# GpSimd's residual DMAs issued behind VectorE's clamp, and a new order at the end of a wkv and binary-FFN kernel

## The chip, the cores and the metric

The kernel runs on one core of a Trainium2 chip. The metric is the device time of one execution in microseconds, the median of the runs shown. PE is TensorE, DVE is VectorE, ACT is ScalarE, POOL is GpSimd, SP is SyncE, which only issues DMAs. All arithmetic on data is in 32-bit floats except the operands of the large matmuls.

## The reference, cut to what matters

```python
x: (4, 1024, 1024); k = v = fside: (4, 1024, 1024)      # batch, time, channel
decay = exp(-exp(w)) * (0.5 + 0.5 * tf)                 # tf = sigmoid(sum(time_emb))
ek = exp(min(k, 30));  ekv = ek * v
nf, df = scan forward  (a = a * decay + ekv,  b = b * decay + ek)
nb, db = scan backward (the same)
euk = exp(min(u + k, 30))
num = nf + nb - ekv + euk * v
den = df + db - ek + euk
wkv = sigmoid(x) * num / max(den, 1e-8) * (0.8 + 0.2 * tf)
bw  = where(weight >= 0, 1, -1) * mean(|weight|, row)
out = x + wkv @ bw.T + bias
```

## The kernel before

**Tiles and steps.** One step n handles one tile of 128 channels by 1024 times; there are 4 batches of CT = 8 tiles, so N = 32 steps, n = 0 to 31. The rows of the profile repeat once per step, some 14.8 us apart. Batches 0 to 2 (24 tiles, 48 half tiles or units, `LAST = 24`) go through the output product inside the step loop, LAG = 9 steps behind; batch 3 is done in natural layout after the loop, in what is called the tail here.

**One step on each engine.** All names with n are semaphores that count finished operations.

- PE transposes k into PSUM `kT` (`k_turn`, 8 matmuls, it waits for VectorE's `own(n-1)`), x into `sT` (`s_turn`), and multiplies units of the product (`unit(u)`, 16 matmuls 128x512) and transposes them back (`turned(u)`, 4 matmuls into `yT`).
- VectorE, in this order: clamp(n) (L715, `pair` to `pair`, both in SBUF), val(n) (L721), own(n) (L722), two forward scans (L683), start values (L696), the backward scan of the numerator, yn(n) (L704), gate(n-1) (L740), the backward scan of the denominator, yd(n) (L704), den(n) (L745, `min(euk, .) + ek`, two inputs in SBUF). L721, L722 and L740 have one input in PSUM.
- ScalarE: ln and rec(n-1), the first guess of 1/den (L556, L558), hi and hib(n-2), the upper half of wkv as a 16-bit float and back (L565, L567), evacuations `evac(u)` (L535) and copies `y_copy(u)` (L544, into `o_nat`), two(n-1) (L591), the exponentials of step n+1 (L524, L525), and in even steps the sigmoids of two x tiles between two loads of activation tables (L607, L609).
- GpSimd: the DMA `ekv += own` of step n-1 (L322), chk(n-1) = euk * rec (L326), which waits for rec(n-1), inv(n-1) (L335), which waits for ScalarE's two(n-1), lo(n-2) (L301), and base(n-1) (L345, wkv times the numerator), which waits for gate(n-1). Clamp(n+1) waits for base(n-1) in turn.

**Residual DMAs.** `residuals(tiles)` (L314) issues on GpSimd, for every finished tile m, a DMA that adds x to `o_nat[m % 4]`. `summed(n)` says which tiles step n takes: none before step 11, one in steps 11 to 31, except steps 27 and 29, which take two (tiles 16 and 17, and 19 and 20), and tile 23 after the loop. Before, the first one stands between chk and inv, the second one behind lo and ahead of base; in steps 17 and 25 (`first`) the order is chk, lo, inv, residual, base. `biases(q)` (L307) issues the DMA that adds the bias to row block q of x, one in each of the steps 3 to 8, behind lo; its x block was loaded by SP (L242) one step earlier. SP stores a tile (L248) once its residual has landed.

**The order of ScalarE's product work** is set by two functions. `made(n)` is how many units PE has multiplied by step n, `cleared(n)` how many ScalarE has evacuated; `clear(lo, hi)` does evac(u) and y_copy(u-1) for each. Before, cleared(29) = 45, cleared(30) = 47, cleared(31) = 48, so evac(47) and y_copy(46) come in step 31, and y_copy(47) after the loop, ahead of `early_out(0)`.

**The tail.** The 16 half rows v of the last batch each need 8 tiles of 2 matmuls, 16 matmuls in all (`across(v, bank, tiles, ...)`). Tiles 0 to 4 are ready early, tile 5 once lo(29) is done, tile 6 with lo(30), tile 7 with `last_lo`. Before the wait on `last_lo` PE does what it can: v = 0 to 7 in the eight banks of PSUM, and v = 8 and 9 into bank 4 (`yT`), from which ScalarE copies them to SBUF (`early_out(0)` and `early_out(1)`, L572). After `last_lo` come the rest, v = 0 to 15 in order. ScalarE's `inverse(31)` (L556, L558) stands behind `early_out(0)`. VectorE ends chk, inv, gate, base and lo of tile 31 itself (L751 to L761), and then scales each half row (L772) and adds x and bias (L776); SP stores each full row block (L285).

Of the kernel before, what the change touches and what calls it, by code (L numbers as in the profile page):

```python
# [39 lines left out]
def bi_wkv_binary_ffn(nc, x, k, cond, w, u, weight, bias, out):  # L40
# [16 lines left out]
    def made(n):  # L57
        return 0 if n < LAG else LATE.get(n, 2 * LAST) if n > N - CT else 2 * (n - LAG + 1)

    def cleared(n):  # L60
        return 0 if n < LAG else made(n) - 1 if n < N - 1 else 2 * LAST

    copied = {u - 1: n for n in range(N) for u in range(cleared(n - 1), cleared(n))}
    copied[2 * LAST - 1] = N - 1
# [7 lines left out]
    with ExitStack() as ctx:  # L72
# [152 lines left out]
        @block.sync  # L225
        def _(sp):
            for p in range(NO):
                sp.sem_inc(o_out[p], 16)
            for i, a in enumerate((w, u, bias)):
                sp.dma_start(rows[i * CT:(i + 1) * CT, :], a.rearrange("(c p) -> c p", p=P)).then_inc(s_par, 16)  # L230
            sp.dma_start(cond4[:, :], cond).then_inc(s_cond, 16)
            sp.wait_ge(s_par, 48)
            sp.wait_ge(s_cond, 16)
            sp.dma_start(k_nat[1][:, :, :], tile_of(k, 1)).then_inc(k_in[1], 16)

            def load_x(n):

                sp.dma_start(x_nat[n % NX][:, :, :], tile_of(x, n)).then_inc(x_in[n % NX], 16)

            def load_tail(q):  # L240

                sp.dma_start(x_tail(q), natural(x, q)).then_inc(t_in[q], 16)  # L242

            def stores(n):
                for m in summed(n):

                    sp.wait_ge(res_in[m % NO], m // NO * 16 + 16)
                    sp.dma_start(tile_of(out_, m), o_nat[m % NO][:, :, :]).then_inc(o_out[m % NO], 16)  # L248

            load_x(0)  # L250
            load_x(1)

            def step(n, p, wt, nxt, nxt3, mid, low, out):
                if wt:

                    done(sp, "sgn", n - 2)
                    done(sp, "abs", n - 2)
                    sp.dma_start(w_nat[p][:, :], weight.rearrange("(o p) i -> o p i", p=P)[n])\
                      .then_inc(w_in[p], 16)
                if n == 0:  # L260
                    load_x(2)
                stores(n - 1)
                if nxt3:

                    done(sp, "kT", n + 1)
                    sp.dma_start(k_nat[1 - p][:, :, :], tile_of(k, n + 3)).then_inc(k_in[1 - p], 16)
                if mid and n + 2 < N:

                    done(sp, "sT", n - 1)
                    load_x(n + 2)  # L270
                if 2 <= n < TT:
                    load_tail(n - 2)
                if n >= N - 2:

                    done(sp, "kT", n)
                    load_tail(TT - N + n)

            out_ = out
            run(None, step)
            stores(N - 1)  # L280
            stores(N)
            for q in range(TT):

                done(sp, "res", 2 * q + 1)
                sp.dma_start(natural(out_, q), x_tail(q)).then_inc(s_tail, 16)  # L285
            for p in range(NO):
                sp.wait_ge(o_out[p], 16 * LAST // NO + 16)
            sp.wait_ge(s_tail, 16 * TT)

        @block.gpsimd  # L290
        def _(pool):
# [25 lines left out]
            def step(n, p, wt, nxt, nxt3, mid, low, out):  # L317
                W, R = wkv[1 - p][:, :], rec[1 - p][:, :]
                if mid:

                    done(pool, "yn", n - 1)
                    pool.dma_start(ekv[1 - p], own[1 - p][:, :], accum_op=ALU.add).then_inc(num_in[1 - p], 16)  # L322

                    done(pool, "rec", n - 1)
                    done(pool, "lo", n - 3)
                    pool.tensor_tensor(W, euk[1 - p][:, :], R, ALU.mult).then_inc(st["chk"], 1)  # L326
                first = n % CT == 1
                if low and first:
                    low_half(n - 2, p)
                if not first:  # L330
                    residuals(summed(n)[:1])
                if mid:

                    done(pool, "two", n - 1)
                    pool.tensor_tensor(W, W, R, ALU.mult).then_inc(st["inv"], 1)  # L335
                if low and not first:
                    low_half(n - 2, p)
                residuals(summed(n) if first else summed(n)[1:])
                if 3 <= n <= TT:
                    biases(n - 3)  # L340
                if mid:

                    done(pool, "gate", n - 1)
# [13 lines left out]
        def _(pe):  # L357
# [123 lines left out]
            done(pe, "own", N - 1)  # L481
            for v in (2, 3):
                across(v, bank[v], range(CT - 3), True, False)
            done(pe, "lo", N - 3)
            for v in range(4):
                across(v, bank[v], range(CT - 3, CT - 2), False, False)
            done(pe, "yc", 2 * LAST - 1)
            across(8, bank[4], range(CT - 2), True, True).then_inc(st["early"], 1)
            s_turn(N - 1)
            pe.wait_ge(st["early_sb"], 1)  # L490
            across(9, bank[4], range(CT - 2), True, True).then_inc(st["early"], 1)
# [9 lines left out]
            for v in range(2 * TT):  # L501
                if v >= 8:
                    done(pe, "res", v - 8)
                tiles = range(CT - 2, CT) if v < 6 or v in (8, 9) else range(CT - 1, CT) if v < 8 else range(CT)
                across(v, bank[v % 8], tiles, v >= 8, True).then_inc(st["nat"], 1)

        @block.scalar
        def _(act):
# [70 lines left out]
            def step(n, p, wt, nxt, nxt3, mid, low, out):  # L579
# [5 lines left out]
                    halves(n - 2, p)  # L585
                if out:
                    clear(cleared(n - 1), made(n - 1))
                if mid:

                    done(act, "chk", n - 1)  # L590
# [30 lines left out]

            run(None, step)

            y_copy(2 * LAST - 1)
            early_out(0)
            inverse(N - 1, 1)
            done(act, "base", N - 2)
# [174 lines left out]
```

## Time and profile before

| | before |
|---|---|
| median of 3 runs | 543.86 us (543.37 to 544.97) |
| the profiled execution | 544.33 us, span of its trace 542.6 us |
| VectorE busy | 504.8 us, 93% |
| ScalarE, GpSimd busy | 378.4 us, 362.3 us |
| PE busy | 363.8 us, granted clock 0.837 on the mean |
| DMA moved | 92.64 MB, 171 GB/s |

Busy time is the sum of the engine's instructions. The chain of the work that ended last (part 4 of the page) lies on VectorE for 59% of the span, and another 22% of it is "issue", time in which the engine that is followed waited for nothing that the profile shows; from 481 us on it lies on PE. An instruction that waits for a port inside its own execution shows that wait as a longer duration and not as idle time before it.

### The profile page before, as it was taken

To read this page: it belongs to the slowest core of one execution; us is meant where nothing else is said; L and a number is where in the kernel's file an instruction comes from. 1 tells how busy PE (TensorE), PEld (TensorE's weight loads), DVE (VectorE), ACT (ScalarE), POOL (GpSimd) and SP (SyncE) were. 2 spreads that over 40 slices of the span, in tenths; PEclk is the share of its full clock that TensorE was granted. 3 is DMA by queue.
4 is the path that set the end of the run, shared out by engine and by line. 5 is a ranking of instruction groups with operands and counts; after the bars stand their busy time and mean duration, and the time that the engine had idled before them with its cause. 6 is when DMAs were issued, how large, how long until landed. Compare 5 with 4: busy or idle time off the path is not lost.

```text
span 542.6 us, 5454 instructions
## 1 busy us (share of the span) xinstructions
PE 363.8 (67%) x1803; PEld 224.1 (41%) x1803; DVE 504.8 (93%) x385; ACT 378.4 (70%) x415; POOL 362.3 (67%) x194
## 2 busy tenths in 40 slices
PE   2233333322578786786786798778799888759996
PEld 1123333312335544444443454554455444524442
DVE  4999999999999999999999999999999999994593
ACT  2849688585859697796969696978889595953100
POOL 0157676667677877777877788877877879873200
PEclk9975655556698798798899878878899999779999
DMA  6745677777633798788899788888779998982942
GB/s 192 196 136 175 195 185 182 206 200 194 155 97 102 148 194 173 163 206 160 157 192 194 153 177 182 185 185 180 180 134 193 216 200 148 195 169 65 185 164 117
DMA packets 125778, 92.64 MB, mean 171 GB/s; under 512 B 2844, under 2 KB 117560, under 8 KB 125752
## 3 DMA queue, kind: packets, MB, share of 16 engines
q0 software_dynamic: 30720, 33.56, 39.2%
q1 hardware_dynamic: 92952, 57.70, 36.0%
q10 hardware_dynamic: 2080, 1.05, 0.7%
q8 instruction: 15, 0.25, 0.2%
q14 instruction: 11, 0.09, 0.1%
HBM read 58.74 MB, written 16.78 MB: 139 GB/s over the span
## 4 chain that ended last, share of the span: by engine, by line
DVE 59%; issue 22%; PE 11%; POOL 5%; DVEq 1%; ACT 1%; DMA 1%; SPq 0%; ACTq 0%
DVE pair L683 25%; DVE pair L704 9%; DVE wkv L740 7%; DVE own L722 6%; POOL wkv L345 5%; DVE pair L721 4%; DVE pair L715 4%; PE sT L420 3%; PE kT L420 3%; PE yT L420 2%; PE prod L420 1%; DVE euk L745 1%; PE cols L420 1%; DVE y_start L696 1%; DMA cond<-in_cond_dram 1%
## 5 line engine op out<-in xcount | busy, mean ns | idle before, releaser
L385 PE MATMUL prod<-acts,sgn 128*128 128x512 f16 x768 | 181.3, 390 | 4.3 <-ACT orow L618 4.0
L704 DVE TENSOR_TENSOR_SCAN pair<-cols,y_start,pair 128x1024 f32<-128x1024 f32 x64 | 150.1, 2346 | 1.1
L363 PE MATMUL kT<-ident,k_nat 128*128 128x128 f32 x256 | 52.1, 371 | 147.1 <-DVE own L722 147.1
L683 DVE TENSOR_TENSOR_SCAN pair<-cols,pair 128x1024 f32<-128x1024 f32 x64 | 142.8, 2272 | 0.0
L326 POOL TENSOR_TENSOR wkv<-euk,rec 128x1024 f32<-128x1024 f32 x31 | 73.1, 2357 | 84.0 <-ACT rec L558 84.0
L385 PEld LDWEIGHTS prod<-acts,sgn 128*128 128x128 f16 (+1 forms) x768 | 77.4, 101 | 90.2 <-issue 9.6
L363 PEld LDWEIGHTS kT<-ident,k_nat 128*128 128x128 f32 x256 | 42.1, 192 | 158.5 <-issue 157.9
L556 ACT ACTIVATE rec<-euk,lnb 128x1024 f32<-128x1024 f32 x32 | 36.8, 1150 | 84.9 <-DVE euk L745 84.8
L335 POOL TENSOR_TENSOR wkv<-wkv,rec 128x1024 f32<-128x1024 f32 x31 | 72.9, 2350 | 18.1 <-ACT wkv L591 18.1
L345 POOL TENSOR_TENSOR wkv<-wkv,pair 128x1024 f32<-128x1024 f32 x31 | 74.1, 2392 | 11.5 <-DVE wkv L740 10.1
L301 POOL TENSOR_TENSOR acts<-wkv,rec 128x1024 f16<-128x1024 f32 x31 | 73.2, 2363 | 9.5 <-ACT rec L567 9.5
L363 PE MATMUL sT<-ident,x_nat 128*128 128x128 f32 x256 | 51.6, 370 | 0.0
L363 PEld LDWEIGHTS sT<-ident,x_nat 128*128 128x128 f32 x256 | 46.2, 199 | 0.4
L745 DVE SCALAR_TENSOR_TENSOR euk<-euk,pair 128x1024 f32<-128x1024 f32 x32 | 43.5, 1360 | 1.1
L363 PE MATMUL yT<-ident,y_fm 128*128 128x128 f32 x192 | 34.0, 307 | 12.3 <-ACT o_nat L544 11.6
L322 POOL DMA_DIRECT2D pair<-own x31 | 29.1, 939 | 19.2 <-DVE pair L704 19.2
L535 ACT ACTIVATE y_fm<-prod,bcol,oscale 128x512 f32<-128x512 f32 x48 | 37.2, 776 | 6.5 <-issue 5.6
L721 DVE TENSOR_TENSOR pair<-pair,kT 128x1024 f32<-128x1024 f32 x32 | 39.0, 1220 | 1.1 <-ACT euk L525 0.3
L591 ACT ACTIVATE wkv<-wkv,two 128x1024 f32<-128x1024 f32 x31 | 35.8, 1155 | 6.0 <-POOL wkv L326 6.0
L722 DVE SCALAR_TENSOR_TENSOR own<-euk,kT 128x1024 f32<-128x1024 f32 x32 | 38.8, 1213 | 0.0
L314 POOL DMA_DIRECT2D o_nat<-in_x_dram x24 | 38.0, 1582 | 0.0
L740 DVE SCALAR_TENSOR_TENSOR wkv<-wkv,sT 128x1024 f32<-128x1024 f32 x31 | 37.0, 1195 | 0.0
(88 smaller groups left out, 502.2 us busy)
## 6 DMA issues: line engine op xcount, KB each, us to landing
x_nat<-in_x_dram SPq DMA_DIRECT2D x32, 512.0 KB, 6.9
pair<-own POOLq DMA_DIRECT2D x32, 512.0 KB, 4.7
k_nat<-in_fside_BxSxS_dram SPq DMA_DIRECT2D x30, 512.0 KB, 3.5
o_nat<-in_x_dram POOLq DMA_DIRECT2D x24, 512.0 KB, 9.1
out_dram<-o_nat SPq DMA_DIRECT2D x24, 512.0 KB, 5.0
y_fm<-in_L_ffn_weight_dram SPq DMA_DIRECT2D x8, 512.0 KB, 5.7
x_end<-in_x_dram SPq DMA_DIRECT2D x6, 512.0 KB, 5.1
x_end<-in_L_ffn_bias_dram POOLq DMA_DIRECT2D x6, 512.0 KB, 6.0
```

What stands on the lines that cost most here:

```text
L301: pool.tensor_tensor(acts[:, 1, n % (2 * CT), :], wkv[p][:, :], rec[p][:, :], ALU.subtract)\
L326: pool.tensor_tensor(W, euk[1 - p][:, :], R, ALU.mult).then_inc(st["chk"], 1)
L335: pool.tensor_tensor(W, W, R, ALU.mult).then_inc(st["inv"], 1)
L345: pool.tensor_tensor(W, W, ekv[1 - p], ALU.mult).then_inc(st["base"], 1)
L363: ins = pe.transpose(dst(q), what(q), one)
L385: ins = pe.matmul(prod[:, h, :], view[:, c, m % CT * P:m % CT * P + P], acts[:, part, m // CT % 2 * CT + c, h * H:(h + 1) * H], start=(par ...
L420: ins = pe.matmul(dst, acts[:, part, LAST // CT % 2 * CT + c, v // 2 * P:(v // 2 + 1) * P], view[:, c, v % 2 * H:(v % 2 + 1) * H], start=( ...
L683: dve.tensor_tensor_scan(buf, d, buf, 0.0, ALU.mult, ALU.add).then_inc(st["F" + kind], 1)
L704: dve.tensor_tensor_scan(buf[:, ::-1], d, buf[:, ::-1], y_start[:, i:i + 1], ALU.mult, ALU.add)\
L721: dve.tensor_tensor(V, E, kT[:, :], ALU.mult).then_inc(st["val"], 1)
L722: dve.scalar_tensor_tensor(own[p][:, :], U, E30, kT[:, :], ALU.min, ALU.mult)\
L740: dve.scalar_tensor_tensor(W, W, HI_SCALE * LO_GAIN / DEN_MIN, sT[:, :], ALU.min, ALU.mult)\
```

## The change

Four things are changed.

1. On GpSimd the first residual DMA of a step now stands right behind the `ekv += own` DMA, with a new wait for clamp(n) ahead of it. The second one (steps 27 and 29), and no other, stands between chk and inv. The bias DMAs of steps 3 to 8 move from behind lo to the same early place, without a wait for the clamp.
2. `cleared(30)` becomes 48: evac(47) and y_copy(46) move to the end of ScalarE's step 30, and y_copy(47) moves into step 31, ahead of two(30).
3. On PE, half row 8 is begun as soon as y_copy(47) is done, with tiles 0 to 4 alone (10 matmuls in place of 12), ahead of the wait for lo(29); its tile 5 is done in the end, where v = 8 now has tiles 5 to 7.
4. The store of the last row block is issued as two halves of 512 columns, the first after half row 14, the second after half row 15.

```diff
     def cleared(n):
-        return 0 if n < LAG else made(n) - 1 if n < N - 1 else 2 * LAST
+        return 0 if n < LAG else made(n) - 1 if n < N - 2 else 2 * LAST
...
-            for q in range(TT):
+            for q in range(TT - 1):
                 done(sp, "res", 2 * q + 1)
                 sp.dma_start(natural(out_, q), x_tail(q)).then_inc(s_tail, 16)
+            for h in range(NH):
+                done(sp, "res", 2 * TT - 2 + h)
+                sp.dma_start(natural(out_, TT - 1)[:, h * H:(h + 1) * H], x_tail(TT - 1)[:, h * H:(h + 1) * H])\
+                  .then_inc(s_tail, 16)
...
                     pool.dma_start(ekv[1 - p], own[1 - p][:, :], accum_op=ALU.add).then_inc(num_in[1 - p], 16)
+                if summed(n):
+                    done(pool, "clamp", n)
+                    residuals(summed(n)[:1])
+                if 3 <= n <= TT:
+                    biases(n - 3)
+                if mid:
                     done(pool, "rec", n - 1)
...
-                if not first:
-                    residuals(summed(n)[:1])
+                residuals(summed(n)[1:])
                 if mid:
                     done(pool, "two", n - 1)
                     pool.tensor_tensor(W, W, R, ALU.mult).then_inc(st["inv"], 1)
                 if low and not first:
                     low_half(n - 2, p)
-                residuals(summed(n) if first else summed(n)[1:])
-                if 3 <= n <= TT:
-                    biases(n - 3)
...
+            done(pe, "yc", 2 * LAST - 1)
+            across(8, bank[4], range(CT - 3), True, True).then_inc(st["early"], 1)
             done(pe, "lo", N - 3)
             for v in range(4):
                 across(v, bank[v], range(CT - 3, CT - 2), False, False)
-            done(pe, "yc", 2 * LAST - 1)
-            across(8, bank[4], range(CT - 2), True, True).then_inc(st["early"], 1)
...
-                tiles = range(CT - 2, CT) if v < 6 or v in (8, 9) else range(CT - 1, CT) if v < 8 else range(CT)
+                tiles = range({6: CT - 1, 7: CT - 1, 8: CT - 3}.get(v, CT - 2) if v < 10 else 0, CT)
...
                     clear(cleared(n - 1), made(n - 1))
+                if n == N - 1:
+                    y_copy(2 * LAST - 1)
                 if mid:
...
             run(None, step)
-            y_copy(2 * LAST - 1)
             early_out(0)
```

GpSimd in step 27, which takes two residual DMAs, from one `ekv += own` DMA (`pair<-own`) to the next. `o_nat<-in_x_dram` is a residual, the four others are chk, inv, lo and base in this order. Before:

```order
L322 DMA pair<-own 128x1024
L326 TENSOR_TENSOR wkv<-euk,rec 128x1024
L314 DMA o_nat<-in_x_dram 128x8x128
L335 TENSOR_TENSOR wkv<-wkv,rec 128x1024
L301 TENSOR_TENSOR acts<-wkv,rec 128x1024
L314 DMA o_nat<-in_x_dram 128x8x128
L345 TENSOR_TENSOR wkv<-wkv,pair 128x1024
L322 DMA pair<-own 128x1024
```

and after:

```order
L327 DMA pair<-own 128x1024
L319 DMA o_nat<-in_x_dram 128x8x128
L338 TENSOR_TENSOR wkv<-euk,rec 128x1024
L319 DMA o_nat<-in_x_dram 128x8x128
L346 TENSOR_TENSOR wkv<-wkv,rec 128x1024
L306 TENSOR_TENSOR acts<-wkv,rec 128x1024
L353 TENSOR_TENSOR wkv<-wkv,pair 128x1024
L327 DMA pair<-own 128x1024
```

Both residuals have moved one place up: the first now runs ahead of chk, the second ahead of inv, and nothing stands between lo and base.

ScalarE from the second table load of step 30 to the first part of `inverse(31)`, with evac (`y_fm<-prod`), y_copy (`o_nat<-yT`), two (`wkv<-wkv,two`) and early_out (`y_fm<-yT`). Before:

```order
L609 ACT_TABLE_LOAD
L556 ACTIVATE rec<-euk,lnb 128x1024
L558 ACTIVATE rec<-rec 128x1024
L565 ACTIVATE acts<-wkv 128x1024
L567 ACTIVATE rec<-acts 128x1024
L535 ACTIVATE y_fm<-prod,bcol,oscale 128x512
L544 COPY o_nat<-yT 128x512
L591 ACTIVATE wkv<-wkv,two 128x1024
L544 COPY o_nat<-yT 128x512
L572 COPY y_fm<-yT 128x512
L556 ACTIVATE rec<-euk,lnb 128x1024
```

and after:

```order
L619 ACT_TABLE_LOAD
L543 ACTIVATE y_fm<-prod,bcol,oscale 128x512
L552 COPY o_nat<-yT 128x512
L564 ACTIVATE rec<-euk,lnb 128x1024
L566 ACTIVATE rec<-rec 128x1024
L573 ACTIVATE acts<-wkv 128x1024
L575 ACTIVATE rec<-acts 128x1024
L552 COPY o_nat<-yT 128x512
L601 ACTIVATE wkv<-wkv,two 128x1024
L580 COPY y_fm<-yT 128x512
L564 ACTIVATE rec<-euk,lnb 128x1024
```

The last evacuation and the copy of unit 46 have moved ahead of the first guess of tile 30, and the copy of unit 47 ahead of two.

PE from the transpose of x tile 30 (`sT<-ident,x_nat`) to the long product of v = 6 and 7 (`sT<-sgn,acts`, 28 matmuls). Before:

```order
L363 MATMUL sT<-ident,x_nat 128x128 x8
L363 MATMUL yT<-ident,y_fm 128x128 x4
L420 MATMUL prod<-sgn,acts 128x512 x10
L420 MATMUL kT<-sgn,acts 128x512 x20
L420 MATMUL prod<-sgn,acts 128x512 x4
L420 MATMUL kT<-sgn,acts 128x512 x4
L420 MATMUL yT<-sgn,acts 128x512 x12
L363 MATMUL sT<-ident,x_nat 128x128 x8
L420 MATMUL yT<-sgn,acts 128x512 x12
L420 MATMUL cols<-sgn,acts 128x512 x12
L420 MATMUL yT<-sgn,acts 128x512 x12
L420 MATMUL sT<-sgn,acts 128x512 x28
```

and after:

```order
L371 MATMUL sT<-ident,x_nat 128x128 x8
L371 MATMUL yT<-ident,y_fm 128x128 x4
L428 MATMUL prod<-sgn,acts 128x512 x10
L428 MATMUL kT<-sgn,acts 128x512 x20
L428 MATMUL yT<-sgn,acts 128x512 x10
L428 MATMUL prod<-sgn,acts 128x512 x4
L428 MATMUL kT<-sgn,acts 128x512 x4
L371 MATMUL sT<-ident,x_nat 128x128 x8
L428 MATMUL yT<-sgn,acts 128x512 x12
L428 MATMUL cols<-sgn,acts 128x512 x12
L428 MATMUL yT<-sgn,acts 128x512 x12
L428 MATMUL sT<-sgn,acts 128x512 x28
```

Half row 8 (the first `yT<-sgn,acts`) has moved ahead of the 8 matmuls that wait for lo(29), and is two matmuls shorter.

## Rows read from the trace of the kernel before

**Rows 1.** The page, part 1: busy time, share of the span, instructions.

```profile
PE 363.8 (67%) x1803; PEld 224.1 (41%) x1803; DVE 504.8 (93%) x385; ACT 378.4 (70%) x415; POOL 362.3 (67%) x194
```

**Rows 2.** The instructions of L745, den: duration in ns min/median/max.

```profile
L745 DVE SCALAR_TENSOR_TENSOR euk<-euk,pair x32: 1224/1226/3369, 22.9 to 489.3; 128x1024 f32<-128x1024 f32 x32
```

**Rows 3.** Timeline (start us, us, instruction, idle before), steps 27 and 29.

```profile
417.95 1.59 POOL L314 DMA_DIRECT2D o_nat<-in_x_dram  x1
...
419.87 2.35 POOL L335 TENSOR_TENSOR wkv<-wkv,rec 128x1024 f32<-128x1024 f32 x1 [0.33 <-ACT wkv L591]
...
422.19 2.36 POOL L301 TENSOR_TENSOR acts<-wkv,rec 128x1024 f16<-128x1024 f32 x1
...
424.50 1.54 POOL L314 DMA_DIRECT2D o_nat<-in_x_dram  x1
425.47 2.96 POOL L345 TENSOR_TENSOR wkv<-wkv,pair 128x1024 f32<-128x1024 f32 x1
426.15 3.37 DVE L745 SCALAR_TENSOR_TENSOR euk<-euk,pair 128x1024 f32<-128x1024 f32 x1
...
457.72 3.35 DVE L745 SCALAR_TENSOR_TENSOR euk<-euk,pair 128x1024 f32<-128x1024 f32 x1
```

**Rows 4.** Timeline, step 26, one residual.

```profile
396.73 1.23 DVE L745 SCALAR_TENSOR_TENSOR euk<-euk,pair 128x1024 f32<-128x1024 f32 x1
397.89 0.74 DVE L715 TENSOR_SCALAR pair<-pair,scl 128x1024 f32<-128x1024 f32 x1
...
400.33 2.36 POOL L326 TENSOR_TENSOR wkv<-euk,rec 128x1024 f32<-128x1024 f32 x1 [2.60 <-ACT rec L558]
...
403.31 1.16 ACT L591 ACTIVATE wkv<-wkv,two 128x1024 f32<-128x1024 f32 x1
...
409.23 2.36 POOL L345 TENSOR_TENSOR wkv<-wkv,pair 128x1024 f32<-128x1024 f32 x1
...
411.45 1.23 DVE L745 SCALAR_TENSOR_TENSOR euk<-euk,pair 128x1024 f32<-128x1024 f32 x1
```

**Rows 5.** Timeline, end of step 3 and start of step 4, weights still being read.

```profile
65.15 0.87 POOL L307 DMA_DIRECT2D x_end<-in_L_ffn_bias_dram  x1
65.16 1.20 DVE L740 SCALAR_TENSOR_TENSOR wkv<-wkv,sT 128x1024 f32<-128x1024 f32 x1
...
68.64 1.23 DVE L745 SCALAR_TENSOR_TENSOR euk<-euk,pair 128x1024 f32<-128x1024 f32 x1
68.73 0.86 POOL L322 DMA_DIRECT2D pair<-own  x1
69.79 0.75 DVE L715 TENSOR_SCALAR pair<-pair,scl 128x1024 f32<-128x1024 f32 x1
```

**Rows 6.** Timeline from step 31 to the first half row of the tail.

```profile
475.82 1.15 ACT L556 ACTIVATE rec<-euk,lnb 128x1024 f32<-128x1024 f32 x1 [0.57 <-DVE euk L745]
...
481.38 1.08 PE L363 MATMUL yT<-ident,y_fm 128*128 128x128 f32 x4 [5.70 <-ACT o_nat L544]
...
489.27 1.23 DVE L745 SCALAR_TENSOR_TENSOR euk<-euk,pair 128x1024 f32<-128x1024 f32 x1
...
494.88 0.59 ACT L572 COPY y_fm<-yT 128x512 f32<-128x512 f32 x1 [11.79 <-PE yT L420]
...
497.63 1.23 DVE L751 SCALAR_TENSOR_TENSOR wkv<-euk,rec 128x1024 f32<-128x1024 f32 x1 [7.13 <-ACT rec L558]
...
499.54 0.57 ACT L572 COPY y_fm<-yT 128x512 f32<-128x512 f32 x1
...
500.73 2.75 PE L420 MATMUL yT<-sgn,acts 128*128 128x512 f16 x12
...
505.63 1.22 DVE L761 TENSOR_TENSOR acts<-wkv,rec 128x1024 f16<-128x1024 f32 x1 [2.21 <-ACT rec L567]
```

**Rows 7.** Busy time by stretch: start:end, length, PE, PEld, DVE, ACT, POOL, clock, DMA, GB/s.

```profile
515.57:538.10 22.53, 22.45 (x105) 9.99 (x102) 16.32 (x26) 0.00 (x0) 0.00 (x0) 1.00 0.36 145
538.10:542.60 4.50, 0.00 (x0) 0.00 (x0) 1.35 (x2) 0.00 (x0) 0.00 (x0) 0.73 0.29 117
```

More of the change, by code:

```diff
@@ L281, in _ @@
             stores(N)
-            for q in range(TT):
+            for q in range(TT - 1):
                 done(sp, "res", 2 * q + 1)
                 sp.dma_start(natural(out_, q), x_tail(q)).then_inc(s_tail, 16)
+            for h in range(NH):
+                done(sp, "res", 2 * TT - 2 + h)
+                sp.dma_start(natural(out_, TT - 1)[:, h * H:(h + 1) * H], x_tail(TT - 1)[:, h * H:(h + 1) * H])\
+                  .then_inc(s_tail, 16)
             for p in range(NO):
                 sp.wait_ge(o_out[p], 16 * LAST // NO + 16)
-            sp.wait_ge(s_tail, 16 * TT)
+            sp.wait_ge(s_tail, 16 * TT + 16)
         @block.gpsimd
```

## The prediction

> **What bounds the kernel now.** I read the busy table first: VectorE is busy 93% of the span, ScalarE, GpSimd and PE about 70% [rows 1]. So inside the steps a gain must come out of VectorE's own instructions or their waits. The instructions by line then show one oddity: den (L745) takes 1.226 us at the median of 32 and 3.369 at most [rows 2]. The timeline has just two such, 3.37 us at 426.15 and 3.35 us at 457.72 [rows 3]; they are the ends of steps 27 and 29, the two with two residual DMAs. There base (L345) ends at 425.47 + 2.96 = 428.43, and den at 429.52, 1.09 us later. In step 26 base ends at 411.59 (409.23 + 2.36) [rows 4]; 1.09 us on is 412.68, just when den ends there undisturbed (411.45 + 1.23). So den, two inputs in SBUF, doesn't read while GpSimd's base reads, and pays for a late base one for one; in all other steps base ends just in time.
>
> In the end VectorE waits: 7.13 us before its chk of tile 31 [rows 6]. That hangs on ScalarE, which sat 11.79 us before `early_out(0)`, from 483.1 to 494.88, for PE, though den(31) had ended at 489.27 + 1.23 = 490.50 and `inverse(31)` stood behind that copy [rows 6]. PE was late as it had idled 5.70 us before turning unit 47 at 481.38, for y_copy(46) [rows 6]. From there PE works on to 538.1: it is 22.45 of 22.53 us busy in the last long stretch, at full granted clock [rows 7]. That stretch is v = 8 to 15 by the program, 4 + 4 + 6 x 16 = 104 matmuls, so 0.2166 us each.
>
> **Part 1, second residual.** In steps 27 and 29 it leaves the place between lo and base. Lo ends at 422.19 + 2.36 = 424.55, so base runs to 426.91 and den, 1.09 later, ends at 428.00 in place of 429.52: 1.52 us. It isn't the whole 2.14, since GpSimd is some 0.6 us late there anyway. Step 29 gives as much. The residual now stands where the first one stood: it ran from 417.95 to 419.54 there, under the wait for two(n-1) that let inv start at 419.87 [rows 3], so it costs nothing. **-3.04 us.** Bounds: 2.4 if base starts 0.3 later each time, 4.3 if den is never disturbed.
>
> **Part 1, first residual** (21 steps, 11 to 31). It leaves a place where inv waits for ScalarE in any case (0.33 us after it [rows 3]): no gain. In its new place, behind the clamp, it starts about 0.08 us after 398.63 (397.89 + 0.74) and needs 1.59, to 400.30; chk started at 400.33 after 2.60 us of waiting [rows 3, 4]. It just fits. Should it be late, chk ends at 402.69 and ScalarE comes to two at 403.31 [rows 4], so 0.6 us more is free. The copies it needs lie in the step before. Queued behind the new wait is chk alone. It now runs beside val and own, which have one input in PSUM like gate (L740), and a DMA issue of GpSimd ran beside gate with 1.20 and 0.87 us for the two [rows 5]. **0 us**, bounds -0.2 and +2 (0.1 in 21 steps).
>
> **Part 1, bias DMAs** (steps 3 to 8). Issued right behind L322 they would run from about 69.6 to 70.5 beside the clamp, at 69.79 to 70.54, while chk comes some 3.6 us after den's start, as at 400.33 after 396.73, so at 72.2 [rows 4, 5]. GpSimd has room for a delay up to 1.7 us. Whether VectorE's clamp is held up no row shows: no DMA issue of GpSimd overlaps a clamp in this trace. The nearest row is L322 at 68.73 beside den at 68.64, with 0.86 and 1.23 us, neither longer than alone [rows 2, 5]. I take **0 us** by that row; the other end is 70.46 less the clamp's real start at 69.87, 0.59 us each, 3.5 us for six.
>
> The Trainium skill speaks against this half: its page "SBUF — State Buffer", section "Who interferes with whom", says that a `tensor_scalar` in a 2-port mode takes the pair of ports shared with GpSimd, that descriptor writing needs them, and that issue order decides who blocks. The clamp is a `tensor_scalar` of 0.75 us, where the same 1024 elements cost den 1.23, so it may well be in such a mode; den has two inputs, for which the page names only GpSimd's reads. By it den beside L322 proves nothing for the clamp, and the sum would be 3.5 us worse; no run here shows it yet.
>
> **Part 2, the end.** ScalarE was free at 475.25 (0.57 us before 475.82 [rows 6]). Evac(47) and y_copy(46) take 1.15 us with their overlap, so ln(30) starts at 476.40, 0.58 late. In step 31 only y_copy(47) stands between hib and two(30) instead of those two, so two(30) keeps its time within 0.1 us, and the rest of step 31 too. PE can turn unit 47 at about 476.55, 4.83 earlier. Its work then, at 0.2166 us per matmul: v = 1 to 479.2, v = 2, 3 to 483.5, the 10 matmuls of v = 8 to 485.7. So `early_out(0)` is over at 486.3, before den(31) ends at 490.50, and ln(31) starts at 490.54 in place of 495.36: all of VectorE's and ScalarE's chain moves 4.82 earlier (chk from 497.63 to 492.8).
>
> PE meanwhile waits for lo(29) at 487.05 (lo ends as base starts, 2.22 before den, by 409.23 and 411.45 [rows 4]), and does its 8 matmuls, x tile 31, v = 9 and v = 5 until 494.9. Then it waits for `early_out(1)`, which was at 499.54 and comes at 494.72 to 495.29. So the 12 matmuls at 500.73 [rows 6] start at 495.4: 5.33 earlier. Nothing behind is later than that: `last_lo`, 506.85 before (505.63 + 1.22), comes at 502.03, while v = 6, 7 keep PE until 504.0. The tail is PE's as before, plus 2 matmuls of v = 8: 0.43 us. **-5.33 + 0.43 = -4.90 us.** If PE runs at half clock for the first ten matmuls, its waits swallow nearly all of it: -4.8. VectorE waited several times in the last rows and stays hidden.
>
> **Part 4, last store.** The DMAs moved for 0.29 of 4.50 us after PE's end [rows 7], 1.3 us for 512 KB; half remains, as the first half goes out 3.4 us earlier. **-0.65 us**, bounds 0 and -1.3.
>
> **Sum.** -3.04 + 0 + 0 - 4.90 - 0.65 = -8.6 us. The profiled execution was 544.33, so 535.7; it stood 0.47 above the median of 543.86, so **535.3**.
>
> **Rivals.**
>
> - *Clamp held up by the bias DMA.* Six times 0.59 = 3.5 us, all on VectorE: 538.8. For it: 0.75 us for the clamp against 1.23 for den shows that the two read differently, so den beside L322 says little. Against it: that pair is still the nearest row, and GpSimd could as well be the one that waits, for free. 20%. The Trainium skill's rule above points the same way, with the order of issue, GpSimd first, as its reason.
> - *The end stays PE's.* If PE doesn't get ahead at 481, because y_copy(46) or own(31) come later than I think, part 2 gives 0 and costs the two matmuls: 535.3 + 4.9 + 0.43 = 540.6. Against it: own(31) ends near 478.9 (den(30) near 475.8, then clamp, val and own, 0.74 + 2 x 1.2, the latter like gate), and ScalarE's free moment is in the rows. 7%.
> - *Slower: GpSimd becomes the bound through the residual's new place.* If descriptor writing beside val and own took twice as long, 3.18 us, chk would come 3.18 - 1.59 - 0.03 = 1.56 late, two 0.96 after its 0.6 of slack, and base is just in time, so den pays 0.96 in each of 21 steps: 20 us, 555.5. It ends slower than 543.9 from a duration of about 2.65 us on, since 8.6 / 21 = 0.41 a step. For it: lo, base and den follow without slack, as steps 27 and 29 show. Against it: gate beside L307. 7%.
> - *It doesn't do what it says:* den at 426 is long for another reason than base, and PE hides the rest: within 0.3%, 3%.
>
> **How the numbers follow.** The forecast gets 63%, with a range of its own of 533.8 to 536.8 (den never disturbed -1.2 and the store's bound; +0.6 and +0.65 the other way, and 0.1 in some steps). The range for 8 in 10 adds the held clamp: 533.8 to 539.2; outside it lie the tail that stays, the slower case and the one without effect, 17%. What a measurement of this kernel can tell from no change is about 0.3%, 1.6 us. Faster: 63 + 20 + 7 = 90%; same: 3%; slower: 7%.
>
> **What the profile after would show.** Den at steps 27 and 29: about 1.8 us each, not 3.4 (1.23 would mean that I have base too late). In steps 3 to 8 clamps of 0.75 as before; clamps of 1.3 would be the first rival. GpSimd's idle time before chk falls from 2.6 to nearly 0 without a later chk. PE turns unit 47 some 4.8 us before the place that it had relative to den(31), no more wait of ScalarE ahead of ln(31), and the first half row of the tail about 5.3 earlier relative to den(31). The stretch after PE's end falls from 4.5 to 3.9 us. I would be wrong if GpSimd's chk were late in most steps, or if the clamps grew.

## The result and the profile after

The changed kernel takes 535.14 us on the median of 4 runs (534.97 to 535.84), the kernel before 543.92 (543.37 to 544.97): a ratio of 0.9839, 95% interval 0.9821 to 0.9856, or 8.8 us less. The profiled execution took 535.84 us, the longest of the four; its span is 534.0 us against 542.6.

Line numbers have moved: on GpSimd chk is now L338, inv L346, lo L306, base L353, the residual L319 and the bias L312, on VectorE the clamp is L724 and den L754, on ScalarE early_out is L580, and `across` on PE is L428.

The four answers below are den's, the clamp's and the bias DMA's instructions, with their duration in ns (min/median/max), and the sign instruction's. The sign instruction turns a tile of the weights into signs; one stands right behind the clamp in each of the steps 0 to 7. They answer to [rows 2] and [rows 5].

```profile
L754 DVE SCALAR_TENSOR_TENSOR euk<-euk,pair x32: 1224/1225/1778, 22.9 to 486.2; 128x1024 f32<-128x1024 f32 x32
L724 DVE TENSOR_SCALAR pair<-pair,scl x32: 740/744/753, 9.8 to 472.7; 128x1024 f32<-128x1024 f32 x32
L312 POOL DMA_DIRECT2D x_end<-in_L_ffn_bias_dram x6: 1359/1359/1362, 54.0 to 130.6; - x6
L698 DVE TENSOR_SCALAR o_nat<-y_fm x8: 665/722/725, 17.5 to 116.5; 128x1024 f16<-128x1024 f32 x8
```

The timeline of GpSimd and VectorE through steps 26 and 27 (start us, us, instruction, idle before) answers to [rows 3, 4]:

```profile
399.06 1.57 POOL L319 DMA_DIRECT2D o_nat<-in_x_dram  x1 [1.21 <-DVE pair L724]
400.45 2.57 POOL L338 TENSOR_TENSOR wkv<-euk,rec 128x1024 f32<-128x1024 f32 x1
404.68 2.36 POOL L346 TENSOR_TENSOR wkv<-wkv,rec 128x1024 f32<-128x1024 f32 x1 [1.65 <-ACT wkv L601]
...
418.08 1.55 POOL L319 DMA_DIRECT2D o_nat<-in_x_dram  x1
420.00 2.35 POOL L346 TENSOR_TENSOR wkv<-wkv,rec 128x1024 f32<-128x1024 f32 x1 [0.37 <-ACT wkv L601]
422.31 2.36 POOL L306 TENSOR_TENSOR acts<-wkv,rec 128x1024 f16<-128x1024 f32 x1
424.64 2.34 POOL L353 TENSOR_TENSOR wkv<-wkv,pair 128x1024 f32<-128x1024 f32 x1
```

```profile
396.87 1.23 DVE L754 SCALAR_TENSOR_TENSOR euk<-euk,pair 128x1024 f32<-128x1024 f32 x1
...
426.29 1.77 DVE L754 SCALAR_TENSOR_TENSOR euk<-euk,pair 128x1024 f32<-128x1024 f32 x1
```

Base follows lo at once in step 27 and den is 1.60 us shorter than its 3.37. The residual in its early place ends at 400.63. Chk's row begins at 400.45, inside that of the residual, and is 0.21 us longer than the 2.36 of [rows 4], so chk ends 6.15 us after den's start where it had ended after 5.96. These 0.19 us vanish before inv, which waits 1.65 us for two.

The end, on ScalarE, PE and VectorE, answers to [rows 6]:

```profile
473.37 1.16 ACT L564 ACTIVATE rec<-euk,lnb 128x1024 f32<-128x1024 f32 x1
...
473.62 0.63 PE L371 MATMUL yT<-ident,y_fm 128*128 128x128 f32 x4 [0.99 <-ACT o_nat L552]
...
480.57 2.32 PE L428 MATMUL yT<-sgn,acts 128*128 128x512 f16 x10
...
482.93 0.58 ACT L580 COPY y_fm<-yT 128x512 f32<-128x512 f32 x1 [3.68 <-PE yT L428]
...
492.30 2.76 PE L428 MATMUL yT<-sgn,acts 128*128 128x512 f16 x12 [0.31 <-ACT y_fm L580]
494.90 6.21 PE L428 MATMUL sT<-sgn,acts 128*128 128x512 f16 x28
500.94 1.89 PE L428 MATMUL prod<-sgn,acts 128*128 128x512 f16 x8
```

```profile
486.24 1.22 DVE L754 SCALAR_TENSOR_TENSOR euk<-euk,pair 128x1024 f32<-128x1024 f32 x1
489.77 1.22 DVE L760 SCALAR_TENSOR_TENSOR wkv<-euk,rec 128x1024 f32<-128x1024 f32 x1 [2.30 <-ACT rec L566]
...
502.00 0.70 DVE L781 TENSOR_TENSOR prod<-prod,orow 128x512 f32<-128x512 f32 x1 [3.01 <-PE prod L428]
...
530.06 0.70 DVE L781 TENSOR_TENSOR sT<-sT,orow 128x512 f32<-128x512 f32 x1 [1.96 <-PE sT L428]
530.79 0.69 DVE L785 TENSOR_TENSOR k_nat<-sT,k_nat 128x512 f32<-128x512 f32 x1
```

PE idles 0.99 us before unit 47 where it had idled 5.70, the first early_out is over before den(31) begins, and VectorE waits 2.30 us before chk, the time that ScalarE's ln and rec of tile 31 take, where it had waited 7.13. The end of the trace comes 2.52 us after VectorE's last instruction (531.48 to 534.0), against 3.12 before. The rows of the kernel before that mark the start of the tail on PE and VectorE's last half row are these:

```profile
509.37 1.89 PE L420 MATMUL prod<-sgn,acts 128*128 128x512 f16 x8
...
538.06 0.70 DVE L772 TENSOR_TENSOR sT<-sT,orow 128x512 f32<-128x512 f32 x1 [1.96 <-PE sT L420]
```

### The profile page after: what moved, and what is told of

The parts are those of the page before. It is cut to its first block, busy times and chain, and to the rows that moved or that the text cites. A ratio compares the mean times of both kernels' runs of the same rounds, so it can differ in the third digit from the quotient of the medians.

```text
span 534.0 us, 5476 instructions
## 1 busy us (share of the span) xinstructions
PE 361.6 (68%) x1803; PEld 222.9 (42%) x1803; DVE 501.8 (94%) x385; ACT 378.5 (71%) x415; POOL 365.0 (68%) x194
## 4 chain that ended last, share of the span: by engine, by line
DVE 61%; issue 23%; PE 8%; POOL 5%; DVEq 1%; ACT 1%; DMA 1%; SPq 0%; ACTq 0%
DVE pair L692 26%; DVE pair L713 10%; DVE wkv L749 7%; DVE own L731 7%; POOL wkv L353 5%; DVE pair L730 5%; DVE pair L724 4%; PE sT L428 3%; PE kT L428 2%; PE yT L428 1%; DVE y_start L705 1%; DVE euk L754 1%; PE cols L428 1%; PE prod L428 1%; DMA cond<-in_cond_dram 1%
## 5 line engine op out<-in xcount | busy, mean ns | idle before, releaser
L346 POOL TENSOR_TENSOR wkv<-wkv,rec 128x1024 f32<-128x1024 f32 x31 | 73.6, 2374 | 39.2 <-ACT wkv L601 39.2
L338 POOL TENSOR_TENSOR wkv<-euk,rec 128x1024 f32<-128x1024 f32 x31 | 78.2, 2524 | 23.0 <-ACT rec L566 23.0
L353 POOL TENSOR_TENSOR wkv<-wkv,pair 128x1024 f32<-128x1024 f32 x31 | 72.9, 2353 | 19.0 <-DVE wkv L749 17.5
L306 POOL TENSOR_TENSOR acts<-wkv,rec 128x1024 f16<-128x1024 f32 x31 | 74.0, 2388 | 4.6 <-ACT rec L575 4.6
L319 POOL DMA_DIRECT2D o_nat<-in_x_dram x24 | 37.8, 1576 | 26.7 <-DVE pair L724 26.7
L754 DVE SCALAR_TENSOR_TENSOR euk<-euk,pair 128x1024 f32<-128x1024 f32 x32 | 40.3, 1260 | 1.1
L327 POOL DMA_DIRECT2D pair<-own x31 | 27.6, 891 | 19.2 <-DVE pair L713 19.2
```

The costliest lines, as they stand in the source:

```text
L306: pool.tensor_tensor(acts[:, 1, n % (2 * CT), :], wkv[p][:, :], rec[p][:, :], ALU.subtract)\
L353: pool.tensor_tensor(W, W, ekv[1 - p], ALU.mult).then_inc(st["base"], 1)
L754: dve.scalar_tensor_tensor(U, U, E30, E, ALU.min, ALU.add).then_inc(st["den"], 1)
```

## The experiments

Each ratio compares a run with the kernel before on the same chip, whose median was 543.92 to 544.86 us. Where a time is set beside the changed kernel's 535.14 us, the two were not measured together, and a difference under 1 us tells nothing, since the medians of the kernel before differ by as much.

### One part at a time

`p1_res_alone` is the kernel before with GpSimd's moves alone. 

> The kernel before with the moves of the residual and bias DMAs on GpSimd alone. Theory: den of steps 27 and 29 falls from 3.37 and 3.35 to 1.77 us, all other dens stay at 1.23, and the bias DMAs cost about 0.14 us together, so the time falls by 3.0 us, to 540.9 with before at 543.9, and VectorE still waits 7.1 us before its chk of tile 31. Rival: the moves do more than that by shorter landings (6.2 us in place of 9.1 in the changed kernel), which would show as a fall of over 4 us; or the steps' gain is given back at the end, under 2 us.

Measured: 540.83 us against 544.15, ratio 0.9929 (0.9905 to 0.9953), 3.3 us less. So the shorter landings, which came here too (6.4 us for the residuals), bring nothing of their own that shows. Two details missed: in the profiled execution (542.51 us, the longest of four) den took 2.17 us in step 27 and 1.77 in step 29, and VectorE's wait before chk of tile 31 was 7.77 us and not 7.1. The 2.17 comes from chk, which begins 4.80 us after den(26) where the changed kernel has 4.18, as it waits for rec; why ScalarE is later there is open.

`p2_end_alone` has ScalarE's and PE's orders alone:

```diff
-        return 0 if n < LAG else made(n) - 1 if n < N - 1 else 2 * LAST
+        return 0 if n < LAG else made(n) - 1 if n < N - 2 else 2 * LAST
...
+                if n == N - 1:
+                    y_copy(2 * LAST - 1)
...
-            y_copy(2 * LAST - 1)
             early_out(0)
...
+            done(pe, "yc", 2 * LAST - 1)
+            across(8, bank[4], range(CT - 3), True, True).then_inc(st["early"], 1)
             done(pe, "lo", N - 3)
...
-            done(pe, "yc", 2 * LAST - 1)
-            across(8, bank[4], range(CT - 2), True, True).then_inc(st["early"], 1)
...
-                tiles = range(CT - 2, CT) if v < 6 or v in (8, 9) else range(CT - 1, CT) if v < 8 else range(CT)
+                tiles = range({6: CT - 1, 7: CT - 1, 8: CT - 3}.get(v, CT - 2) if v < 10 else 0, CT)
```

> The kernel before with ScalarE's and PE's new order at the end alone (parts 2 and 3), the store whole. Theory: -4.9 us, to 539.0: ln(31) starts right behind den(31), VectorE's wait before chk of tile 31 falls from 7.1 to 2.3 us, the 12 matmuls ahead of the 28 start 5.3 us earlier, and the tail is 0.43 us longer by two matmuls. Den of steps 27 and 29 stays at 3.4. Rival: with the dens still long the ScalarE order gives another amount, as steps 27 and 29 are the ones that set GpSimd's and ScalarE's distance there: under 4 us.

Measured: 539.28 us, ratio 0.9899 (0.9874 to 0.9924), 4.9 us less; the wait before chk is 2.31 us, den still takes 3.37 at most. The two add up to 8.2 of 8.8 us, each with some 1.3 us of uncertainty. The store was not run alone, but the traces show it: from VectorE's last instruction to the end it is 3.09 to 3.16 us in the six with the whole store (the kernel before, p1 to p4, q3), and 2.48 to 2.56 in the seven with the two halves.

`p3_act_alone` is the first three pieces of that diff (ScalarE's order), `p4_pe_alone` the last three (PE's).

> The kernel before with ScalarE's new order alone, PE in its old order. Theory, from the changed kernel's rates: PE turns unit 47 some 4.8 us earlier but waits for lo(29) before v = 8, which then ends near den(31) + 0.9 us, so ln(31) starts some 1.5 us after den(31) ends, and all behind it too. The tail starts about 2.1 us later than with both and is 0.43 us shorter: -3.2 us, to 540.7. Rival: ScalarE's order is the whole of it, and PE's order gives nothing: -4.9.

> The kernel before with PE's new order alone, ScalarE in its old one. Theory: PE still turns unit 47 at 481.4 and works without a gap from there to 538, so that moving two matmuls behind and one group ahead changes nothing at the end: within 0.4 us of before, though ln(31) starts about 2.1 us earlier and VectorE's wait before chk falls from 7.1 to 5.0 us. Rival: VectorE's chain sets the end, and the time falls by about 2 us with it.

Measured: p3 542.54 us on the median of 10 runs (540.76 to 544.13), ratio 0.9961 (0.9947 to 0.9976), 1.6 us less and not 3.2. p4 544.07 us, ratio 0.9993 (0.9980 to 1.0006): nothing, as expected, though VectorE's wait before chk fell from 7.1 to 5.6 us there (5.0 expected), and its wait for the first half row rose from 3.58 to 5.29. So the end hung on PE and not on VectorE's chain. The shares aren't additive: 1.6 and 0 apart, 4.9 together. PE's timeline in p3's profiled execution, at 544.13 us the longest of its ten, shows one reason:

```profile
479.31 4.48 PE L420 MATMUL kT<-sgn,acts 128*128 128x512 f16 x20
...
487.39 1.89 PE L420 MATMUL prod<-sgn,acts 128*128 128x512 f16 x4 [3.60 <-POOL acts L301]
...
489.07 1.91 PE L420 MATMUL kT<-sgn,acts 128*128 128x512 f16 x4
...
490.78 3.78 PE L420 MATMUL yT<-sgn,acts 128*128 128x512 f16 x12
```

and the stretches of p3 (start:end, length, PE, PEld, DVE, ACT, POOL, granted clock, DMA, GB/s), the wait and what follows it:

```profile
483.70:487.30 3.60, 0.09 (x1) 0.00 (x0) 3.60 (x3) 0.00 (x0) 3.60 (x3) 0.82 1.12 142
487.30:490.70 3.40, 3.31 (x8) 1.20 (x9) 3.37 (x2) 0.00 (x0) 3.20 (x3) 0.50 0.54 154
490.70:494.30 3.60, 3.60 (x13) 1.47 (x12) 0.02 (x1) 0.00 (x0) 0.00 (x0) 0.70 0.77 146
```

Left without work for 3.60 us, PE comes back at a granted clock of 0.50, the lower of its two levels (1.2 GHz): the two groups of 4 matmuls take 1.9 us each where the changed kernel's take 1.0, and the 12 take 3.78 for 2.75. That is 2.8 us on the engine that sets the end. With both orders the ten matmuls of v = 8 fill most of that wait, and the clock stays at 1.00:

```profile
473.60:482.90 9.30, 9.26 (x44) 4.29 (x44) 9.16 (x7) 5.58 (x6) 7.51 (x4) 1.00 0.73 113
482.90:484.05 1.15, 0.01 (x1) 0.02 (x2) 1.15 (x2) 0.58 (x1) 1.11 (x2) 1.00 0.96 290
484.05:491.90 7.85, 7.85 (x40) 3.94 (x40) 5.48 (x4) 4.34 (x5) 3.22 (x3) 1.00 0.39 77
```

The runs of p3 lie 3.4 us apart, the fastest (540.76) just where my theory had it and the median 1.8 us above. That the clock doesn't fall, or falls for a shorter time, in some of them would fit, but one trace can't show it.

### Why den was long

`q3_den_psum`, on the kernel before, takes den's second SBUF input away in steps 27 and 29:

```diff
-                dve.scalar_tensor_tensor(U, U, E30, E, ALU.min, ALU.add).then_inc(st["den"], 1)
+                if isinstance(n, int) and n in (27, 29):
+                    done(dve, "expU", n + 1)
+                    dve.scalar_tensor_tensor(U, U, E30, kT[:, :], ALU.min, ALU.max).then_inc(st["den"], 1)
+                else:
+                    dve.scalar_tensor_tensor(U, U, E30, E, ALU.min, ALU.add).then_inc(st["den"], 1)
```

> The kernel before, with den of steps 27 and 29 taking its second input from kT in PSUM in place of ek in SBUF (max in place of the sum, so the denominators of these two tiles are other numbers), behind ScalarE's exponentials. Theory: den is long because its second SBUF input waits for base on GpSimd, so it falls to 1.23 us in both steps. The clamp behind it waits for base by a semaphore, so only part of the 2.1 us is won: clamp starts near base's end + 0.1, about 0.9 us earlier, 1.8 us in all, 542.1. Rival: den waits for something else that is late then (DMA issue, a queue), and stays at 3.4 us with the time of before.

```profile
425.42 2.97 POOL L345 TENSOR_TENSOR wkv<-wkv,pair 128x1024 f32<-128x1024 f32 x1
426.10 1.22 DVE L747 SCALAR_TENSOR_TENSOR euk<-euk,kT 128x1024 f32<-128x1024 f32 x1
...
428.50 0.75 DVE L715 TENSOR_SCALAR pair<-pair,scl 128x1024 f32<-128x1024 f32 x1 [1.17 <-POOL wkv L345]
```

Base is as late as before, yet den takes 1.22 us beside it: it was the second SBUF input that waited for GpSimd's instruction. The clamp then shows the same lateness openly, as 1.17 us of waiting. The time is 541.43 us against 544.13, ratio 0.9952 (0.9936 to 0.9969): 2.7 us and not 1.8. The two traces show where the rest is. Step 27 gives 0.95 us (clamp at 428.50 for 429.45), but step 29 gives 1.50: chk begins 3.59 us after den(28) there and not 4.18, so base ends 1.68 us after den's start in place of 2.27. And PE's ten matmuls after unit 47 took 3.45 us, where the profiled execution of the kernel before has 3.94 and that of p1 4.47. In all three PE had idled 5.1 to 6.3 us before, and over the first 4.6 to 4.7 us of this work the granted clock was 0.65, 0.55 and 0.50. So up to 1 us comes and goes there from run to run.

`q2_res_before_base` puts all residual DMAs where the second one had been, on the changed kernel:

```diff
-                if summed(n):
-                    done(pool, "clamp", n)
-                    residuals(summed(n)[:1])
...
-                residuals(summed(n)[1:])
...
                 if low and not first:
                     low_half(n - 2, p)
+                residuals(summed(n))
```

> The changed kernel with all residual DMAs between lo and base, where the second one of steps 27 and 29 stood before; the bias DMAs as in the changed kernel. Theory: base comes some 1.5 us late in each of the 21 steps and den is held as long, 2.6 to 3.4 us in place of 1.23, for some 30 us more, near 565. Rival: den was long in steps 27 and 29 for a reason of those steps (three units of the product in the step before, DMA traffic) and stays at 1.23 in the steps with one residual; then the time is within 5 us of 535.

Measured in a single run: 565.25 us, 30 more than the changed kernel.

```profile
L750 DVE SCALAR_TENSOR_TENSOR euk<-euk,pair x32: 1224/2646/4355, 22.7 to 514.7; 128x1024 f32<-128x1024 f32 x32
```

Half of all dens are now longer than 2.6 us, and each of the long ones that I compared ends 1.09 or 1.10 us after its base (base to 401.01, den to 402.10). Only in steps 17 and 25, where the order differs and base waits for gate in any case, is den 1.23 us. So den pays for a late base in any step, and steps 27 and 29 aren't special.

### What the wait for the clamp is for

`q1_no_clamp_wait` is the changed kernel without the line `done(pool, "clamp", n)`.

> The changed kernel without GpSimd's wait for the clamp: the first residual DMA follows the ekv DMA at once and so is issued beside the clamp. Theory: as the bias DMAs beside the clamp showed in the changed kernel (1.36 us for 0.87, clamp 0.75 as ever), VectorE isn't held and GpSimd is, by some 0.5 to 0.7 us; the residual then ends no later than it does behind the wait, chk is on time, and the time is that of the changed kernel within 0.5 us, 535.1. Rival A: the longer residual DMA holds the clamp, 0.4 us or more in 21 steps, over 8 us slower. Rival B: it is held far longer than the clamp lasts, chk comes late by more than 0.6 us, and den pays.

Measured: 546.41 us against 544.13, ratio 1.0042 (1.0025 to 1.0059), and 11.3 us slower than the changed kernel. My theory fell. The clamp's instructions, and one of them with the residual beside it:

```profile
L723 DVE TENSOR_SCALAR pair<-pair,scl x32: 744/1317/1340, 9.7 to 483.1; 128x1024 f32<-128x1024 f32 x32
```

```profile
421.43 2.18 POOL L319 DMA_DIRECT2D o_nat<-in_x_dram  x1
...
421.89 1.32 DVE L723 TENSOR_SCALAR pair<-pair,scl 128x1024 f32<-128x1024 f32 x1
```

Clamp 1.32 in place of 0.745 us: 0.57 in each of 21 steps is 12.0 us. Against that, no den is longer than 1.24 us here, which gives 1.1 back; den(31) begins 11.0 us later than in the changed kernel. Chk isn't late; it still waits 0.7 us for rec. So rival A holds. But the bias DMAs are issued in just that way beside the clamp and leave it at 0.75 us; between them and the residuals the pieces differ, 4 KB against 512 B. `q5_rows` is the kernel of q1 and changes only these:

```diff
-                    pool.dma_start(o_nat[m % NO][:, :, :], tile_of(x, m), accum_op=ALU.add)\
+                    pool.dma_start(o_nat[m % NO][:, :, :].rearrange("p q f -> p (q f)"),
+                                   x[m // CT, (m % CT) * P:(m % CT + 1) * P, :], accum_op=ALU.add)\
```

> As q1_no_clamp_wait (no wait for the clamp), but the residual DMA adds a block of 128 whole rows of x, 4 KB in a piece for each partition, in place of the 128x8x128 tile in pieces of 512 B: the same bytes, an eighth of the pieces, so a wrong residual in batches 0 to 2. Theory, formed on the run without the wait (clamp 1.32 us in place of 0.75 beside a residual issue of 2.18, but 0.75 beside a bias issue of 1.36): what holds the clamp is the writing of many pieces; with the bias DMA's number of them the issue takes 1.4 us, the clamp 0.75, and the time is near 535. Rival: it is the place in the step, or the batches' other work, and the clamp stays at 1.3 us, near 546.

Measured: 536.13 us, ratio 0.9851 (0.9811 to 0.9891).

```profile
398.13 1.34 POOL L319 DMA_DIRECT2D o_nat<-in_x_dram  x1
...
398.61 0.74 DVE L724 TENSOR_SCALAR pair<-pair,scl 128x1024 f32<-128x1024 f32 x1
```

The same bytes at the same place in 4 KB pieces: the clamp is 0.74 us and the 10 us are gone. So what holds VectorE goes with the pieces. In the changed kernel, where the small pieces are issued behind the clamp, val and own beside them keep their 1.22 and 1.21 us, so it matters that the issue meets the clamp. Whether the number of descriptors that GpSimd writes does it, their size or the first transfers, no run separates.

How long GpSimd is held is less than the durations say, since the row of an issue right behind another issue begins before that one ends. In q5's tail, with no clamp near, it begins 0.29 us early and shows 1.18 us:

```profile
495.05 0.88 POOL L319 DMA_DIRECT2D o_nat<-in_x_dram  x1
495.64 1.18 POOL L312 DMA_DIRECT2D k_nat<-in_L_ffn_bias_dram  x1
```

Counted from the end of the issue before, a bias DMA takes 0.89 us there and 1.08 beside the clamp (54.29 to 55.37 in the changed kernel), and q1's residual takes 1.89 (421.72 to 423.61) where one behind the clamp takes 1.57. GpSimd loses 0.2 and 0.3 us, VectorE nothing and 0.57.

The Trainium skill, page "SBUF — State Buffer", section "Who interferes with whom", says that the first of the two to start gets the shared ports for its whole instruction and the other blocks fully. Of den against base that holds here in each trace. Of the clamp against the residual DMA it holds in part: both grow, the DMA by 0.3 us and the clamp from 0.745 to 1.32, and the clamp ends at 423.21, before the DMA does, so neither was blocked for the whole of the other. The bias DMA begins before the clamp (54.29 and 54.50) and doesn't block it at all.

`q4_bias_old` is the changed kernel with the bias DMAs back behind lo.

> The changed kernel with the bias DMAs of steps 3 to 8 back behind lo. Theory: the bias DMAs take 0.87 us again, the sign instruction behind the clamp 0.69 in place of 0.72, and VectorE reaches step 26 some 0.14 us earlier; nothing that the time can show. Rival: the 0.14 us stays, as it has another cause.

Measured in one run: 535.61 us. The bias DMAs take 0.866 us, the sign instruction 0.685 where it had 0.722, and den of step 25 begins at 396.65 and not at 396.87. Of these 0.22 us, 0.12 stand there before the first bias DMA counts (den of step 2 at 53.23 and 53.35). The bias DMAs' place costs the changed kernel 0.10 to 0.14 us, and in each of the five steps with signs behind the clamp the sign instruction is 0.037 us longer. The rival falls.

### A faster version

`r1_two_first` is the changed kernel with ScalarE's two ahead of the first evacuation in steps 27 and 29:

```diff
-                if out:
+                if out and n not in (27, 29):
                     clear(cleared(n - 1), made(n - 1))
...
+                if out and n in (27, 29):
+                    clear(cleared(n - 1), made(n - 1))
                 if nxt:
                     exps(n + 1, 1 - p)
```

> The changed kernel with one more move on ScalarE: in steps 27 and 29 the first evac and y_copy come behind two. Theory: what is left of den there (1.77 and 1.78 us) is ScalarE's lateness after the three units of the step before; two now comes when chk ends, inv follows the second residual's end 0.35 us earlier than before, and den falls to about 1.4 us each: 0.7 us less in all, 534.4. Rival: evac's delay hits PE and comes back; no gain or a loss.

`r2_all` adds the bias DMAs' old place and a fuller PE at the end:

```diff
             across(8, bank[4], range(CT - 3), True, True).then_inc(st["early"], 1)
+            pe.wait_ge(st["early_sb"], 1)
+            across(9, bank[4], range(CT - 3), True, False)
             done(pe, "lo", N - 3)
+            across(9, bank[4], range(CT - 3, CT - 2), False, True).then_inc(st["early"], 1)
...
-            pe.wait_ge(st["early_sb"], 1)
-            across(9, bank[4], range(CT - 2), True, True).then_inc(st["early"], 1)
...
+            for v in (6, 7):
+                across(v, bank[v], range(CT - 2), True, False)
             done(pe, "lo", N - 2)
             for v in (6, 7):
-                across(v, bank[v], range(CT - 1), True, False)
+                across(v, bank[v], range(CT - 2, CT - 1), False, False)
...
             early_out(0)
+            early_out(1)
             inverse(N - 1, 1)
```

> As r1_two_first, with the bias DMAs back behind lo and PE's waits at the end filled: half row 9 begins with tiles 0 to 4 right behind early_out(0), its tile 5 comes with lo(29), early_out(1) comes ahead of inverse(31), and v = 6 and 7 take tiles 0 to 5 before they wait for lo(30). Theory: PE's waits of 1.1 us (lo(29)) and 0.3 us (early_out(1)) shrink to 0.5 in all, the tail starts 0.9 us earlier relative to den(31); with 0.7 and 0.14 from the steps 1.8 us in all, 533.3. Rival: VectorE's chain to last_lo takes over as the bound, or PE's clock falls; gain under 1 us.

Measured: r1 534.28 us, ratio 0.9813 (0.9797 to 0.9829), r2 533.13 us, ratio 0.9792 (0.9776 to 0.9808), against 544.86 for before. R1's interval overlaps the changed kernel's 0.9821 to 0.9856, so its gain isn't shown; in its profiled execution den of step 27 even took 2.17 us and that of step 29 1.44. As in p1, chk was late for rec in step 27, 5.01 us after den(26). R2 lies clear of it, by 2.0 us by the medians and 0.5% by the ratios. Its dens take 1.44 and 1.43 us as expected, and at the end:

```profile
485.29 1.23 DVE L759 SCALAR_TENSOR_TENSOR euk<-euk,pair 128x1024 f32<-128x1024 f32 x1
...
500.10 0.70 DVE L786 TENSOR_TENSOR prod<-prod,orow 128x512 f32<-128x512 f32 x1 [2.06 <-PE prod L428]
```

From den(31)'s end to the first half row it is 13.58 us, where the changed kernel has 14.54 (487.46 to 502.00): 0.96, for an expected 0.9.

## Why the prediction was right

The forecast was 535.3 us and the measured median 535.14. Its terms, each as the two profiled executions show it (that of the kernel before at 544.33 us, that of the changed one at 535.84):

| term | forecast | measured |
|---|---|---|
| den of steps 27 and 29 | -3.04 | 3.37 + 3.35 to 1.77 + 1.78: -3.17 |
| first residual's new place | 0 | 0 (inv 7.81 us after den, 7.83 before) |
| bias DMAs | 0 | den(25) at 396.87 for 396.73: +0.14 |
| end of den(31) to the start of the tail on PE | -5.33 | 18.87 to 13.48: -5.39 |
| two more matmuls: start of the tail on PE to VectorE's last L772 (now L781) | +0.43 | 28.69 to 29.12: +0.43 |
| last store: VectorE's end to the end | -0.65 | 3.12 to 2.52: -0.60 |
| sum | -8.6 | -8.6 (span 542.6 to 534.0) |

That the medians agree to 0.2 us is luck in part. The rows of den and of the bias DMAs miss by -0.13 and +0.14 and cancel; den of step 27 took 2.17 us in p1 and r1 against 1.77, and PE's ten matmuls after unit 47 took 3.45 to 4.47 us in kernels with ScalarE's old order, so either row could have come out 0.4 or 0.5 us off. One sum of the prediction is wrong without effect: 535.3 - 1.2 - 0.65 is 533.4 and not 533.8, the lower end of its range.

**Second residual.** That den pays one for one for a late base was read from two instructions; q3 (den without its second SBUF input: 1.22 us beside the same base) and q2 (30 us for residuals in that place in all steps) show it as the cause. That 0.6 us would stay was right (0.54 did). The prediction put it down to GpSimd, which is late in these steps anyway; what makes it late is ScalarE, whose rec lets chk begin 4.2 us after den's start in place of 3.6, and r2, with two in an earlier place, takes 0.34 of each den away.

**First residual.** It fitted, with 0.2 us less room than I had, out of the 0.6: the residual starts 0.30 us behind the clamp's end (399.06) and not 0.08. The slower rival, its issue stretched beside val and own, didn't come: it takes 1.57 us there. I hadn't seen what the wait for the clamp is worth: without it the move costs 11.3 us more and the kernel would have been slower than before (q1). My row for a DMA issue beside den, and later the bias DMAs beside the clamp, spoke for few large pieces alone.

**Bias DMAs.** The rival had six clamps held for 0.59 us each. The clamps stayed at 0.745 us and the issue's row grew to 1.36, of which 0.2 us is delay; 0.14 us came in the steps with sign instructions, which I had left out. The residual DMA shows that the rival was no idle one: 1024 pieces hold a clamp for 0.57 us. That this is near the rival's 0.59 is a coincidence, for that was the overlap with an issue of 0.87 us.

**The end.** The gain was PE's, as the prediction had it, with VectorE's chain moved 4.83 us for 4.82 (its wait from 7.13 to 2.30). P3 and p4 show that neither order does it alone. The prediction's remark that a half clock at the start would be swallowed didn't get its test, for the clock stayed at 1.00 in the changed kernel. In p3 it fell later, after the wait for lo(29), with no wait behind it, and cost 2.8 us.

## What to carry to other kernels

A VectorE instruction with two SBUF inputs beside GpSimd's elementwise work hides its wait in its own duration, so compare its longest with its median; a DMA issue of GpSimd is paid there by pushing the next elementwise instruction into it. Issue scattered DMAs from GpSimd outside an instruction like the clamp here (one input, both sides in SBUF, 0.745 us where den takes 1.23), or in large pieces: a wait that costs nothing can be worth 11 us. Take the delay of a GpSimd issue from its end and not from its duration, when another issue stands right before it. At an end bound by PE, what counts is when PE starts and that it doesn't run dry, and two reorderings may be worth 0 and 1.6 us apart and 4.9 together.

## What was unexpected of the hardware

- A GpSimd DMA issue of 1024 pieces of 512 B beside a `tensor_scalar` of 0.745 us delays both, itself by 0.3 us and the `tensor_scalar` by 0.57. One of 4 KB pieces and the same 512 KB leaves the `tensor_scalar` at 0.74 and is itself delayed by 0.2; the sign instruction behind it takes 0.722 us for 0.685.
- In p3's trace PE came back at half its clock after 3.60 us without work, which cost 2.8 us of an expected gain of 3.2; in the changed kernel, after 1.15 us, it hadn't dropped.
- Landing of the residual DMA fell from 9.1 to 6.2 us in its new place, and of the x tiles from 6.9 to 4.9 (6.0 to 7.3 in the four other traces with the old place), while the mean traffic stayed (171 and 173 GB/s). That of the bias DMA rose from 6.0 to 7.8. No term of the time hung on it.
